# Expert layer on one core: first parameters ahead of the first gathers, later ones behind the scatter-adds, products begun with the first two chunks, the last full tiles by halves

## The chip, the cores and the metric

The kernel runs on one core of a Trainium2 chip. The metric is the device time of one execution in microseconds (us); less is better. Three executions of the kernel before took 483.40, 480.20 and 482.25 us, median 482.25. One further execution was profiled: 481.19 us, of which the span from the program's first instruction to its last is 479.5.

## The reference, cut to what matters

4096 tokens of 256 values pass through a mixture of 8 experts of three layers, and each token takes the two experts of the largest gate weights. All is float32.

```
var  = mean(x * x);  xn = rms_w * (x * rsqrt(var + 1e-6))
gate = xn @ wg_W + wg_b + (genre @ gg_W + gg_b)
w    = softmax(gate); the two largest are kept         # cw
h1   = relu(x @ W1[e] + b1[e])                         # 256 -> 512
h2   = relu(h1 @ W2[e] + b2[e])                        # 512 -> 512
out  = x + sum over the two experts of cw * (h2 @ W3[e] + b3[e])
```

## The kernel before

**Routing.** Tokens are sorted by expert, so that each expert is computed for its own tokens alone. The first 48 us work out the gates, choose two experts for each token, give every (token, expert) pair a slot and turn slots into tokens by products with one-hot matrices (L1167, eight batches of eight matmuls, `s_inv`). Behind each batch but the last stand four warm-up matmuls (`keep_busy(WARM_BATCH)`), behind the last one 96. The result is `tab_from` (L1001), the row of `x_ext` that each slot reads, and later `tab_to`, the row of the output that it adds to. `x_ext`, in DRAM, holds each token with its eight gate weights behind it; the gate weights (`dense`) are stored there by two DMAs that ACT's queue issues (L731), the token values by SP's queue.

**Experts are ranked by size.** `experts_of_tiles` (L966 to L979, VectorE, signal `s_names`) writes the rank of the expert of each tile into `etile`; rank 0 is the largest expert. Weights of rank 0 are loaded, scaled and split first. A float32 weight is split into two float16 parts: ScalarE writes the high part (`high_parts`, L716), VectorE the low part (`low_parts`, L825, two operations for each chunk). Each product is then three float16 matmuls (high by high, high by low, low by high). The activations are split in the same way (`split`, L1023 and L1025).

**Tiles.** 36 tiles of 256 slots follow. 32 of them have one expert each; three in the middle (29 to 31, `paired`) carry two experts of 128 slots each, whose weights are copied into `stage` (L1050), and the last, 35, is one half. One step of TensorE is, for tile i: layer two of tile i (48 matmuls of 256 columns), layer one of tile i+1 (24), the transposes of tile i+2 (four, L1182), layer three of tile i (24, L1260; by halves L1273, and L1286 in the last tile). Layer two waits for both halves of the split of `h1` (`s_h1`, `2 * i + 2`), layer three for both of `h2`. A half of a split is two of four chunks of 128 hidden units; ScalarE's activations (L770) deliver them chunk by chunk from the banks.

**The other engines in step i.** ScalarE: activations of layer two of tile i, of layer one of tile i+1, the high part of x for tile i+2, in some steps weight scales, high parts and sums of squares of a later expert, then the weighing of y (L780). VectorE: splits of both, the low part of x (L1012), in some steps two `low_parts`, then `finish` (L1030; by halves L1039), which takes y out of the bank. GpSimd: copies the table columns of tiles i and i+3 (L574), issues the two gathers of tile i+3 (L579), in some steps computes the parameters of a later expert (`parameters(late)`, L519 to L536, fourteen short operations linked by a semaphore), copies the parameters of tile i+2 (L588, awaited by the activations of its first layer), waits until tile i is weighed and the previous scatter-adds have landed, copies the gate weights of tile i+2 (L599) and issues the two scatter-adds of tile i to the output (L611). `PARAMETERS_AT` says in which step which rank is computed: ranks 1 to 7 in steps 0, 3, 6, 9, 12, 15 and 18.

**Start.** GpSimd waits for `x_ext` and `tab_from`, gathers tiles 0 and 1, computes the parameters of rank 0, waits for `s_names`, copies the parameters of both tiles and gathers tile 2. TensorE transposes tile 0 when its gathers have landed, runs 24 warm-up matmuls, layer one of tile 0, the transposes of tile 1, 24 more warm-ups, and enters step 0.

## Time and profile before

| | |
|---|---|
| median of three executions | 482.25 us |
| the profiled execution, its span | 481.19 us, 479.5 us |
| TensorE matmuls | busy 431.3 us, 90% of the span |
| VectorE, ScalarE, GpSimd | busy 306.3, 289.9 and 302.3 us |
| layers one and two, full tiles (L1226) | 2304 matmuls, ordinary spacing 0.109 us |
| layer three, full tiles (L1260) | 744 matmuls |
| scatter-adds (L611) | 71, mean 1679 ns, 3.9 us from issue to landing |
| gathers (L579) of tiles 3 on | 65, 3.0 us from issue to landing |

Times in the rows count from the start of the span. A matmul's recorded end is modelled and lies behind the start of the next, so a full TensorE is told by the starts. GpSimd's ends are rough. A value in square brackets is the idle time of the engine just before, with what ended it. Where one instruction waits for several semaphores, the wait is put down to the one that came last.

### The profile page before, as it was taken

What the parts mean: (1) busy time and instruction counts of PE and PEld (TensorE: products, weight loads), DVE (VectorE), ACT (ScalarE), POOL (GpSimd) and SP (SyncE); (2) the same over time, 40 slices, a digit from 0 to 9 for tenths busy, and PEclk for the clock granted to TensorE, in tenths of its full rate; (3) what the DMA queues carried; (4) which work ended last, traced back from release to release, by engine and by line L of the source; (5) the groups of instructions that cost most, each with busy time, mean ns of one, the idle gap of its engine ahead of it and who ended that gap; (6) DMA issues with size and microseconds to landing.
All of it is one profiled execution on the core that took longest, in us unless ns stands there. A gap on an engine that the chain in (4) does not pass through costs nothing.

```text
span 479.5 us, 13384 instructions
## 1 busy us (share of the span) xinstructions
PE 431.3 (90%) x4296; PEld 385.7 (80%) x4296; DVE 306.3 (64%) x531; ACT 289.9 (60%) x608; POOL 302.3 (63%) x457
## 2 busy tenths in 40 slices
PE   7606889999899999999999999899999999999980
PEld 6406768998689889888888998788899999899870
DVE  4898734776657756856856666555566667775550
ACT  6606529877578768778777764544555556554550
POOL 5720742757777776877877776766656666666451
PEclk9956989999899999999999999999999999999997
DMA  8989692555434544240444331322323433112221
GB/s 289 352 227 377 255 327 82 129 151 135 118 71 131 135 68 122 40 68 24 60 73 115 63 61 22 69 47 46 46 46 51 56 46 47 26 24 40 35 34 19
DMA packets 27179, 49.48 MB, mean 103 GB/s; under 512 B 8267, under 2 KB 21645, under 8 KB 24941
## 3 DMA queue, kind: packets, MB, share of 16 engines
q0 software_dynamic: 13632, 18.00, 22.9%
q1 hardware_dynamic: 9280, 30.45, 18.0%
q8 instruction: 42, 0.69, 0.6%
q10 hardware_dynamic: 4205, 0.17, 0.5%
q14 instruction: 20, 0.16, 0.1%
HBM read 40.08 MB, written 17.83 MB: 121 GB/s over the span
## 4 chain that ended last, share of the span: by engine, by line
PE 37%; POOL 26%; issue 12%; DVE 7%; ACT 5%; POOLq 4%; DMA 2%; DVEq 1%; SPq 0%; ACTq 0%
PE bank L1226 25%; POOL out L611 11%; PE bank L1260 7%; POOL area L579 5%; POOL bound L519 2%; ACT area L756 2%; DMA stage<-in_weights 1%; POOLq L597 1%; DVE area L1025 1%; PE bank L1202 1%; POOL cfrom L574 1%; DVE area L1023 1%; PE bank L1182 1%; ACT area L770 1%; PE bank L1273 1%
## 5 line engine op out<-in xcount | busy, mean ns | idle before, releaser
L1226 PE MATMUL bank<-area,w_hi 128*128 128x256 f16 x1536 | 257.0, 275 | 6.2 <-DVE area L1025 5.8
L1226 PE MATMUL bank<-area,w_lo 128*128 128x256 f16 x768 | 210.8, 274 | 0.0
L770 ACT ACTIVATE area<-bank,cprm 128x256 f32<-128x256 f32 (+1 forms) x264 | 132.3, 556 | 78.2 <-PE bank L1226 62.1
L1226 PEld LDWEIGHTS bank<-area,w_hi 128*128 x1536 | 150.7, 99 | 26.3 <-issue 8.2
L1023 DVE CAST area<-area 128x512 f16<-128x512 f32 (+1 forms) x144 | 66.1, 459 | 137.4 <-ACT area L770 127.1
L611 POOL DMA_INDIRECT out<-area,cto x71 | 119.2, 1679 | 41.9 <-issue 29.3
L1025 DVE TENSOR_TENSOR area<-area 128x512 f16<-128x512 f32 (+1 forms) x144 | 99.0, 688 | 5.0
L579 POOL DMA_INDIRECT area<-x_ext,cfrom x65 | 69.6, 1071 | 37.7 <-POOL cfrom L574 27.9
L1260 PE MATMUL bank<-w_hi,area 128*128 x496 | 86.3, 273 | 0.0
L1226 PEld LDWEIGHTS bank<-area,w_lo 128*128 x768 | 75.8, 99 | 9.3
L780 ACT ACTIVATE area<-area,cw 128x256 f32<-128x256 f32 x71 | 32.3, 500 | 71.0 <-DVE area L1030 52.7
L1260 PE MATMUL bank<-w_lo,area 128*128 x248 | 67.6, 273 | 0.0
L1260 PEld LDWEIGHTS bank<-w_hi,area 128*128 128x128 f16 x496 | 48.5, 98 | 5.3
L574 POOL COPY cto<-tab_to 128x2 int32<-128x2 int32 x36 | 33.0, 916 | 0.0
L599 POOL COPY cw<-area 128x2 f32 (+1 forms) x39 | 10.9, 282 | 33.4 <-ACT area L780 24.4
L1012 DVE SCALAR_TENSOR_TENSOR area<-bank,small,area 128x512 f16<-128x512 f32 x36 | 26.8, 746 | 3.1 <-ACT area L744 2.9
L744 ACT ACTIVATE area<-bank,small 128x512 f16<-128x512 f32 x36 | 24.9, 692 | 4.3 <-PE bank L1182 4.3
L574 POOL COPY cfrom<-tab_from 128x2 int32<-128x2 int32 x33 | 27.1, 820 | 0.0
L1202 PE MATMUL bank<-area,stage 128*128 128x128 f16 x432 | 25.1, 219 | 1.9 <-DVE area L1025 1.2
L1260 PEld LDWEIGHTS bank<-w_lo,area 128*128 128x128 f16 x248 | 24.3, 98 | 2.8
L1202 PEld LDWEIGHTS bank<-area,stage 128*128 128x128 f16 x432 | 24.4, 98 | 2.5 <-issue 2.4
L1182 PE MATMUL bank<-ident,area 128*128 128x128 f32 x142 | 21.6, 274 | 4.4 <-DMA area<-x_ext,cfrom 2.6
(199 smaller groups left out, 468.9 us busy)
## 6 DMA issues: line engine op xcount, KB each, us to landing
stage<-in_weights SPq DMA_DIRECT2D x10, 1024.0 KB, 6.0
area<-in_x SPq DMA_DIRECT2D x8, 512.0 KB, 7.5
x_ext<-in_x SPq DMA_DIRECT2D x8, 512.0 KB
out<-in_x SPq DMA_DIRECT2D x8, 512.0 KB, 6.9
w_lo<-in_weights SPq DMA_DIRECT2D x4, 1024.0 KB, 8.3
w_hi<-in_weights SPq DMA_DIRECT2D x2, 1024.0 KB, 9.0
out<-area,cto POOLq DMA_INDIRECT x71, 3.9
area<-x_ext,cfrom POOLq DMA_INDIRECT x65, 3.0
```

The costliest lines, as they stand in the source:

```text
L574: pool.tensor_copy(to, table[:, bass.ds(i * SUB, SUB)]).then_inc(signal, 1)
L579: pool.indirect_dma_start(out=xg[:, s, u, :], out_offset=None, in_=x_ext, in_offset=bass.IndirectOffsetOnAxis(ap=rows[:, u:u + 1].bitcast( ...
L611: pool.indirect_dma_start(out=out, out_offset=bass.IndirectOffsetOnAxis(ap=cto[:, s, u:u + 1].bitcast(U32), axis=0), in_=yb[:, s, u, :], i ...
L770: ins = act.activation(to[:, m * T + u * wide:m * T + (u + 1) * wide], ps_h[layer][b][:, a * T + u * wide:a * T + (u + 1) * wide], ACT.Rel ...
L780: act.activation(yb[:, slot, u, :], y32[:, u * H:(u + 1) * H], ACT.Copy, scale=cw[:, slot, u:u + 1]).then_inc(s_y, 1)
L1012: dve.scalar_tensor_tensor(xt_lo, ps_x[:, :], sx, xt_hi, ALU.mult, ALU.subtract).then_inc(s_xs, 1)
L1023: dve.tensor_copy(hi_b, h_b).then_inc(half_done, 1)
L1025: dve.tensor_tensor(lo_b, h_b, hi_b, ALU.subtract).then_inc(signal, 1)
L1182: ins = nc.tensor.transpose(ps_x[:, k * T + u * P:k * T + (u + 1) * P], xg[:, slot, u, k * P:(k + 1) * P], ident[:, :])
L1202: ins = nc.tensor.matmul(banks[u][:, m * P:(m + 1) * P], own[u][(0, 0, 1)[n]][:, at_own:at_own + P], xp[:, cols], start=(k == 0 and n == 0 ...
L1226: ins = nc.tensor.matmul(banks[m // 2][:, (m % 2) * T + u * wide:(m % 2) * T + (u + 1) * wide], weight, xp[:, cols], start=(k == 0 and n = ...
L1260: ins = nc.tensor.matmul(ps_y[:, u * H:(u + 1) * H], hp[:, cols], wp[:, bass.ds(w[u % len(w)] + (W3_AT + k * H), H)], start=(k == 0 and n ...
```

## The change

- **Parameters.** Rank 0's are computed before GpSimd waits for `x_ext` and `tab_from`, and tile 0's and 1's copies follow right behind the gathers of their tile. In the steps, the late parameters stand at the end, behind the scatter-adds; rank 1's move from step 0 to step 1.
- **Names.** The first four tiles (`FIRST`) take rank 0 as a constant, so that nothing waits for `s_names` before tile 4, and VectorE runs `experts_of_tiles` behind the low parts of the first expert instead of ahead of them.
- **Gate weights.** Their two stores to `x_ext` go from ACT's queue to SP's, behind the loads of rank 0's weights and bias and ahead of rank 1's.
- **Products.** Layer two of a full tile starts at the first half of `h1`: chunks 0 and 1 for output blocks 0 and 2, then, after the second half, the rest. Layer three does the same in all tiles but the paired ones: both halves of the tile with chunks 0 and 1, then both with 2 and 3. For that y lies in two banks.
- **End.** Tile 33 is finished, weighed and added by halves too.
- **Warm-up.** Four matmuls behind each of the first three batches only.

```diff
+FIRST = -(-LEAST // E)
-LOWS_AT, SQUARES_AT, SUMS_AT, HIGHS_AT, PARAMETERS_AT = {1: 2, 2: 3}, {}, {}, {0: 2, 1: 3}, {0: 1}
+LOWS_AT, SQUARES_AT, SUMS_AT, HIGHS_AT, PARAMETERS_AT = {1: 2, 2: 3}, {}, {}, {0: 2, 1: 3}, {1: 1}
...
-            return i + pair(i) + (1 if i > LAST - 1 else 0)
+            return i + pair(i) + max(0, i - (LAST - 2))
-            return paired(i) or i == LAST - 1
+            return paired(i) or i >= LAST - 2
...
-        bank = [ctx.enter_context(nc.psum_tensor(f"bank{b}", [P, 512], F32)) for b in range(8)]
+        bank = [ctx.enter_context(nc.psum_tensor(f"bank{b}", [P, 512], F32)) for b in range(5)]
+        y_banks = ctx.enter_context(nc.psum_tensor("y_banks", [P, SUB, 512], F32))
+        bank += [y_banks[:, u, :] for u in range(SUB)]
+        bank.append(ctx.enter_context(nc.psum_tensor("bank7", [P, 512], F32)))
...
# SP, behind b3_rows(e)
+                if e == 0:
+                    sp.wait_ge(s_dense, 1)
+                    for h in range(2):
+                        first = h * (N // 2 + 1)
+                        sp.dma_start(x_ext[first:first + N // 2, H:ROW].rearrange("(p j) e -> p j e", j=J),
+                                     je(dense)[h * P // 2:(h + 1) * P // 2]).then_inc(s_ext, 16)
...
# GpSimd, copy_parameters
+                if i == FIRST:
+                    pool.wait_ge(s_names, 1)
-                    e = pool.value_load(etile[0:1, bass.ds(name_at(i, u), 1)], min_val=0, max_val=E - 1)
+                    e = 0 if i < FIRST else \
+                        pool.value_load(etile[0:1, bass.ds(name_at(i, u), 1)], min_val=0, max_val=E - 1)
# GpSimd, step
-                if late is not None:
-                    link(parameters(late))
                 if i + 2 == PAIRED_AT:
                     pool.wait_ge(s_wsq, 4 * E)
...
                 add_rows(i, s)
-
+                if late is not None:
+                    link(parameters(late))
+
+            pool.wait_ge(s_whole, 1)
+            pool.wait_ge(s_order, 1)
+            link(parameters(0))
             pool.wait_ge(s_ext, (OUT_PARTS + 4) * 16)
             pool.wait_ge(s_from, 1)
             experts_of = []
             for i in range(RING):
                 gather(i, i, tab_from[:, i * SUB:(i + 1) * SUB])
-                if i == 1:
-                    pool.wait_ge(s_whole, 1)
-                    pool.wait_ge(s_order, 1)
-                    link(parameters(0))
-                    pool.wait_ge(s_names, 1)
-                    for n in range(2):
-                        experts_of.append(copy_parameters(n, n))
+                if i < 2:
+                    experts_of.append(copy_parameters(i, i))
...
# ScalarE, start
-            act.wait_ge(s_dense, 1)
-            for h in range(2):
-                first = h * (N // 2 + 1)
-                act.dma_start(x_ext[first:first + N // 2, H:ROW].rearrange("(p j) e -> p j e", j=J),
-                              je(dense)[h * P // 2:(h + 1) * P // 2]).then_inc(s_ext, 16)
...
# VectorE, behind tab_from
-            experts_of_tiles()
             low_parts(0)
+            low_parts(1, (0,))
             tables()
-            low_parts(1, (0,))
             x_low(0)
             low_parts(1, (1,))
+            experts_of_tiles()
             split(0, 0)
...
# TensorE
-                if b < BATCHES - 1:
+                if b < SUMS_BEHIND_BATCH:
                     keep_busy(WARM_BATCH, ones16[:, :], bank[6])
...
+                early, late = (0, 1), (2, 3)
+                pe.wait_ge(s_h1, 2 * i + 1)
+                products(*tile, 0, early)
+                products(*tile, 2, early)
+                pe.wait_ge(s_h1, 2 * i + 2)
+                products(*tile, 0, late)
+                products(*tile, 1, early + late).then_inc(s_l2, 1)
+                products(*tile, 2, late)
+                products(*tile, 3, early + late).then_inc(s_l2, 1)
...
# TensorE, start
-            pe.wait_ge(s_names, 1)
             layer1(0, weights_at(0))
```

`products` is new: it runs the three matmuls for each of the chunks `ks` into output block m. Layer three becomes what `layer3_last` was, with y in the two banks, for every tile that is not paired.

## Rows read from the trace of the kernel before

**Rows 1.** The page's first line.
```profile
span 479.5 us, 13384 instructions
```

**Rows 2.** Waits of TensorE: line <- releaser: us in total, times, longest.
```profile
PE bank L1226 <- DVE area L1025: 5.8, 7, 2.1
PE bank L1182 <- DMA area<-x_ext,cfrom: 2.6, 2, 1.7
```

**Rows 3.** Windows: stretch, length, busy time (count) by engine, clock, DMA share, GB/s.
```profile
54.00:55.80 1.80, 0.01 (x1) 0.01 (x1) 0.93 (x1) 0.01 (x1) 1.65 (x2) 1.00 0.32 94
66.30:69.70 3.40, 3.40 (x18) 2.42 (x17) 0.00 (x0) 0.08 (x1) 1.91 (x2) 0.50 0.90 301
122.24:124.20 1.96, 0.00 (x0) 0.00 (x0) 1.93 (x4) 1.93 (x5) 1.66 (x2) 1.00 0.01 1
124.35:127.70 3.35, 3.35 (x17) 2.42 (x16) 3.35 (x4) 0.99 (x2) 2.81 (x3) 0.50 0.59 74
303.18:304.85 1.67, 0.00 (x0) 0.00 (x0) 1.57 (x4) 1.11 (x3) 1.67 (x1) 1.00 0.27 51
```

**Rows 4.** Timeline of the front: start, us, engine, line, operation, [idle before].
```profile
27.69 5.39 ACTq L731 DMA_DIRECT2D x_ext<-area  x2
...
45.15 0.30 ACT L708 ACTIVATE scale<-expo,act_bias 128x3 int32<-128x3 int32 x1
...
48.04 0.23 DVE L1001 TENSOR_SCALAR tab_from<-bank 128x72 int32<-128x72 f32 x1 [1.90 <-PE bank L1167]
...
49.20 1.25 POOL L579 DMA_INDIRECT area<-x_ext,tab_from  x1 [19.35 <-DVE tab_from L1001]
...
50.44 2.48 DVE L825 SCALAR_TENSOR_TENSOR w_lo<-stage,scale,w_hi 128x1024 f16<-128x1024 f32 x2
...
50.75 1.79 POOL L579 DMA_INDIRECT area<-x_ext,tab_from  x1 [0.30 <-issue]
...
55.82 0.63 PE L1182 MATMUL bank<-ident,area 128*128 128x128 f32 x4 [1.81 <-DMA area<-x_ext,tab_from]
...
65.25 0.39 PE L1226 MATMUL bank<-area,w_hi 128*128 128x256 f16 x2 [2.11 <-DVE area L1025]
```

**Rows 5.** Timeline of GpSimd, step 0: first and last operation of `parameters`.
```profile
77.28 0.30 POOL L519 TENSOR_SCALAR bound<-fsq,small 128x1 f32<-128x1 f32 x1 [8.65 <-ACTq L710]
...
80.86 0.19 POOL L536 TENSOR_TENSOR prm<-prm,inv_scale 128x1 f32<-128x1 f32 x1
```

**Rows 6.** Timeline of step 1: weighing of tile 1 and its first scatter-add.
```profile
91.92 0.91 ACT L780 ACTIVATE area<-area,cw 128x256 f32<-128x256 f32 x2
...
94.63 1.79 POOL L611 DMA_INDIRECT out<-area,cto  x1 [0.40 <-issue]
```

**Rows 7.** Timeline of steps 15 to 17, GpSimd with its neighbours.
```profile
250.51 2.17 POOL L519 TENSOR_SCALAR bound<-fsq,small 128x1 f32<-128x1 f32 x1
...
253.35 0.91 ACT L780 ACTIVATE area<-area,cw 128x256 f32<-128x256 f32 x2
...
256.39 0.18 POOL L536 TENSOR_TENSOR prm<-prm,inv_scale 128x1 f32<-128x1 f32 x1
...
261.99 2.47 DVE L825 SCALAR_TENSOR_TENSOR w_lo<-stage,scale,w_hi 128x1024 f16<-128x1024 f32 x2
...
265.35 1.04 POOL L579 DMA_INDIRECT area<-x_ext,cfrom  x1 [0.85 <-POOL cfrom L574]
266.70 0.98 POOL L579 DMA_INDIRECT area<-x_ext,cfrom  x1 [0.31 <-issue]
...
269.80 0.60 PE L1182 MATMUL bank<-ident,area 128*128 128x128 f32 x4
```

**Rows 8.** Timeline of the end: layer three of tile 34, scatter-adds of tiles 34 and 35.
```profile
460.54 0.28 PE L1273 MATMUL bank<-w_hi,area 128*128 x1 [1.19 <-DVE area L1025]
...
464.34 1.58 POOL L611 DMA_INDIRECT out<-area,cto  x1 [2.94 <-DMA out<-area,cto]
...
470.87 1.55 POOL L611 DMA_INDIRECT out<-area,cto  x1 [2.90 <-ACT area L780]
```

More of the change, by code:

```diff
@@ L317, in build_moe @@
         ps_h = [[bank[0], bank[1]], [bank[2], bank[3]]]
[L318 to L320 removed]
+        ps_x, ps_y = bank[4], y_banks[:, :, 0:H]
         s_const = sem("s_const")
@@ L1241, in layer1 @@
                 pe.wait_ge(s_xs, i + 1)
-                layer(w, P if paired(i) else T, owned(i, 0), W1_AT, KH, (xt_hi, xt_lo), ps_h[0], s_l1,
-                      copied=(s_own1, pair(i) * SUB + 1), ready=[(s_xs, i + 1)] * 2 if two(i) else None)
+                own, copied = owned(i, 0), (s_own1, pair(i) * SUB + 1)
+                if two(i):
+                    halves_of_layer(own, KH, (xt_hi, xt_lo), ps_h[0], s_l1, copied, [(s_xs, i + 1)] * 2)
+                    return
+                if paired(i):
+                    pe.wait_ge(*copied)
+                tile = (w[0], halves_of(i) * P, own and own[0], W1_AT, KH, (xt_hi, xt_lo), ps_h[0])
+                for m in range(KM):
+                    ins = products(*tile, m, range(KH))
+                    if m % 2:
+                        ins.then_inc(s_l1, 1)
             def layer2(i, w):
@@ L1247, in layer2, with layer3_pair @@
                     wait_lows(pe, 1)
-                if not two(i):
-                    pe.wait_ge(s_h1, 2 * i + 2)
-                layer(w, P if paired(i) else T, owned(i, 1), W2_AT, KM, (h1_hi, h1_lo), ps_h[1], s_l2,
-                      copied=(s_own2, pair(i) * SUB + 1), ready=[(s_h1, 2 * i + 1 + u) for u in range(2)] if two(i) else None)
-            def layer3(i, w):
-                pe.wait_ge(s_h2, 2 * i + 2)
+                own, copied = owned(i, 1), (s_own2, pair(i) * SUB + 1)
+                if two(i):
+                    halves_of_layer(own, KM, (h1_hi, h1_lo), ps_h[1], s_l2, copied,
+                                    [(s_h1, 2 * i + 1 + u) for u in range(2)])
+                    return
+                if paired(i):
+                    pe.wait_ge(*copied)
+                tile = (w[0], halves_of(i) * P, own and own[0], W2_AT, KM, (h1_hi, h1_lo), ps_h[1])
+                early, late = (0, 1), (2, 3)
[7 more added lines that the diff above has]
+                products(*tile, 3, early + late).then_inc(s_l2, 1)
+            def layer3_pair(i, w):
                 pe.wait_ge(s_y32, pieces_before(i) + 1)
                 for u in range(SUB):
+                    pe.wait_ge(s_h2, 2 * i + 1 + u)
                     for k in range(KM):
```

70 lines of the change are left out of this document (23 added, 47 removed).

## The prediction

> **What bounds the kernel now.** I read the span first [rows 1], then the waits of TensorE alone [rows 2], then windows over each longer wait [rows 3]. The reader is to see that TensorE is the bound from tile 0's second layer on (65.25 [rows 4]) to the end: its second-layer products wait 5.8 us in all, in seven places, and its transposes 2.6 us, in two. Every other microsecond there can shrink only if a matmul is taken away, and the change takes none away in the tiles. So the change can win in three places: ahead of 65.25, in those few waits, and in the tail.
>
> A wait has a second price. The granted clock was 1.00 while TensorE stood from 122.24 to 124.20, and 0.50 for the next 3.4 us, all of them full of matmuls; the same after the 2.11 us before 65.25 [rows 3, 4]. At half of 2.4 GHz 3.4 us do the work of 1.7, so each cost 1.7 us more. Waits of 1.80 us (54.00) and 1.67 us (303.18) were followed by no fall [rows 3]. The Trainium skill (TensorE: Matmul & The Clock Gate, Part 1) says the gate follows how busy the array has lately been; by that a 1.7 us stall may cost nothing more or another 1.7, according to what lies around it. No run here varies it.
>
> The chain of waits behind those stalls is GpSimd's. One tile costs it two gathers, a copy of parameters and two scatter-adds; a step with `parameters(late)` costs it 3.8 us more when VectorE leaves it alone (77.28 to 81.05 [rows 5]) and 6.1 us when two of VectorE's low parts lie beside it (250.51 to 256.57; its first operation, 0.30 us elsewhere, took 2.17 [rows 5, 7]).
>
> **1. The front.** Parameters of expert 0 now come ahead of the first gather. They can start when ScalarE has the scales, 45.45 [rows 4], or up to 1 us sooner, since the store of the gate weights, whose issue ran until 33.08, no longer runs ahead of the weights; nothing to 1, taken 0.5. From about 45 to 46 VectorE makes one-hots; `tab_from` (48.04) comes earlier, since 12 warm-up matmuls between the last batches go: at most by the 1.90 that VectorE waited for those batches [rows 4], by 1.0 if each took 0.05 to 0.1, so at 47.1; and VectorE, which now leaves `experts_of_tiles` (48.27 to 50.44 [rows 4]) for later, starts its low parts at once: three of 1.24 us, 47.3 to 51. So parameters meet exactly the neighbour that slowed them at 250.51. Alone they would end at 49.3 and the first gather start at 50.2; with each low part holding up one operation they end near 52, and the gather starts near 53, against 49.20. The Trainium skill (SBUF — State Buffer, "Who interferes with whom") has the two engines share an exclusive lock held for a whole instruction, and advises putting on the far side of it whichever is off the critical path. By it this move is wrong, and 53 is the figure; without it 50.2.
>
> Before, the second gather (50.75) was found landed at 55.82, 5.1 us later, with weights in flight; the later steady ones need at most 3.1 (266.70 to 269.80 [rows 7]). A second gather at 54.3 lands after 3.1 to 3.7: 57.4 to 58. Transposes are then 1.6 to 2.2 us late. Against that, tile 0's first activation no longer waits for the parameter copy, and layer two starts when TensorE has issued what lies between: before, 2.11 of the 9.43 us from 55.82 to 65.25 were idle [rows 4]. 7.3 us after 57.7 is 65.0. `experts_of_tiles` has been put ahead of tile 0's split and ends it no later than that. Layer two thus starts 0.2 us earlier: I take zero. The clock: the 2.11 us wait and its 1.7 us go, but TensorE now stands some 4 us (53.5 to 57.7) instead of 1.8, longer than the waits that were followed by half a clock. I let the two cancel. Bounds: 3.8 us won (gather at 50.2, no fall of the clock) and 3.8 lost (gather later by another 2 us, clock lost twice).
>
> The store of gate weights, moved to SP's queue, took ACT's queue 5.39 us to issue [rows 4], with ScalarE waiting for weights anyway. On SP it stands behind expert 0's weights, so expert 1's and 2's are issued up to 5 us later. ScalarE takes expert 1's up after four conversions of expert 0's (some 4 us from 45.5): covered; without that cover, up to 2 us, inside the bounds. The first gather waits for this store too; at 53 it has landed. No wait for names before tile 4: nothing, cover ample.
>
> **2. Late parameters go behind the scatter-adds.** Take the step whose tile is weighed at 254.26 [rows 7]. In waiting steps the first scatter-add starts 1.8 us after the weighing (92.83 to 94.63 [rows 6]): 256.1. Two of 1.8 and 1.6 with a gap of 0.3 [rows 6, 8] end at 259.8. Parameters follow, then the next step's table copies (0.3), the gather's lead (0.85) and the second gather 1.35 behind the first [rows 7]. VectorE's next two low parts (261.99 to 264.46, about 1 us earlier in the new order) lie right on the parameters. So they end between 263.6 (3.8 us) and 265.9 (6.1); the second gather starts at 266.1 to 268.4, against 266.70; it lands 3.1 later, 269.2 to 271.5. TensorE wants it at 269.5 (269.80 less 0.3 of wait that goes). The stall is 0 to 2.0 us. The low parts are there in each cycle, so I go by the upper row, and take 1.5 because GpSimd's ends are rough and what follows a scatter-add begins before its recorded end.
>
> It recurs in all seven such steps (1, 3, 6, 9, 12, 15, 18), since each counts from the tile before: 10.5 us, and 0.5 for gathers that meet weights in flight: 11.0. It stands against what goes: tile 5's wait (1.96) with its clock (1.7), the other five waits of that line (5.8 - 2.1 - 2.0 = 1.7), of which starting with the first two chunks removes what the early copy of parameters would leave, and both transposes' waits (2.6), which turn into the new ones: 8.0. Net **+3.0**. What is queued behind the late parameters is the gather of tile i+4; before, it was the scatter-add of tile i, which nobody awaits.
>
> **3. First chunks first, y in two banks.** Same matmuls, 0.109 us apart. Layer two may start 1.1 us before its second split ends, layer three likewise. In the middle the waits it can take are already counted. Layer two's first half is signalled after 30 of 48 matmuls, not 24, hidden by the next tile's first layer.
>
> **4. The end.** The 1.19 us before tile 34's layer three go (460.54 [rows 8]). But the last scatter-add (470.87) waits for tile 34's to have landed as well as for its own tile; those start at 464.34, once tile 33's have landed and tile 34 is weighed. Tile 33 by halves frees the first condition by 1.5 us; the second moves 0.3 to 0.6, as VectorE still splits tile 35 in between. Won: 0.5 (0 to 1.3).
>
> **Sum**, from the profiled execution's own 481.2 (span 479.5): 0 + 3.0 - 0.2 (small waits among the pairs) - 0.5 = +2.3: **483.5**. That execution lies 1.1 us under the median of the runs.
>
> **Rivals.**
> - *GpSimd keeps up.* If parameters take nearer 3.8 us, the gathers land before 269.5 and the 8.0 us go for nothing: 481.2 - 8.0 - 0.5 = 472.7. For it: 3.8 is measured, and low parts may slip past. Against: at 250.51 they did not. 0.28.
> - *The stalls halve the clock* (slower). Place: transposes of tiles 5, 7, 10, 13, 16, 19, 22. It decides from stalls of about 1.96 us, seen to be followed by half a clock; 1.80 was not. At 2.0 us in seven places, three of them with 1.7 more: 14 + 5.1 - 8.5 = +10.6, 491.8; with one, 488.4. 0.22.
> - *The front decides*: late parameters neutral in total, front at either bound: 478 or 487. 0.05.
> - The forecast, 480 to 487: 0.45.
>
> **Numbers.** About 1% (4.8 us) is what a measurement tells from no change. Faster by more (under 477.4): the first rival, 0.28. Slower by more (over 487.1): most of the second, 0.22. Within: 0.50. Range 474 to 490: it leaves out the lower half of the first rival and the top of the second. The forecast's own is 480 to 487.
>
> **What would show it.** TensorE's waits: transposes waiting for gathers in about seven places, 1 to 2 us each, tile 5's layer-two wait gone. GpSimd: parameters of expert 0 ending near 52 and the first gather near 53; later ones of about 6 us, with single operations over 1 us. Clock at half near 57 instead of 66. I am wrong if transposes hardly wait (then fast), if parameters run in 4 us beside low parts, or if layer two of tile 0 starts more than 2 us from 65.

## The result, and the profile after

| | before | after |
|---|---|---|
| median of the runs, us | 482.03 (4 runs, 480.2 to 483.4) | 500.34 (4 runs, 497.32 to 501.82) |
| profiled execution, us (its span) | 481.19 (479.5) | 497.32 (495.7) |
| mean granted clock in it | 0.961 | 0.948 |

The ratio is 1.0374, 95% interval 1.0309 to 1.0439: slower by 18 us. The forecast was 483.5 with a range of 474 to 490, so it was wrong, and the time lies beyond even the rival that comes nearest (491.8). The profiled execution is the fastest of the four runs after; it shows 16.1 us of the 18. Ratios, here and below, leave out disturbed executions, so they can differ a little from those of the medians.

The page's first line of the kernel after, and TensorE's waits (line <- releaser: us in total, times, longest), against [rows 1, 2]:

```profile
span 495.7 us, 13085 instructions
```
```profile
PE bank L1188 <- DMA area<-x_ext,cfrom: 17.3, 7, 4.5
...
PE bank L1188 <- DMA area<-x_ext,tab_from: 5.9, 1, 5.9
...
PE bank L1212 <- DVE area L1031: 1.1, 1, 1.1
PE y_banks L1293 <- DVE area L1031: 0.9, 1, 0.9
```

The layer-two waits (5.8 us in seven places) are gone altogether. In their place the transposes (now L1188) wait for gathers seven times, 17.3 us. I followed them in the timeline of TensorE: 110.47 (2.31), 134.81 (1.92), 170.32 (2.18), 207.50 (2.18), 244.61 (2.11), 280.06 (2.12) and 319.17 (4.47), the transposes of tiles 5, 7, 10, 13, 16, 19 and 22, each the first that needs a gather issued behind late parameters.

Windows over two of them (stretch, length, then busy time and count for PE, PEld, DVE, ACT and POOL, clock, DMA share, GB/s), against [rows 3]:

```profile
108.16:110.47 2.31, 0.00 (x1) 0.01 (x1) 0.37 (x1) 1.42 (x4) 2.14 (x4) 1.00 0.32 93
110.47:113.90 3.43, 3.43 (x31) 3.13 (x32) 3.36 (x6) 3.25 (x6) 2.37 (x4) 1.00 0.51 58
...
168.14:170.32 2.18, 0.00 (x0) 0.00 (x1) 0.38 (x1) 1.43 (x4) 2.00 (x4) 1.00 0.31 103
170.95:174.70 3.75, 3.75 (x22) 2.73 (x20) 1.97 (x4) 3.39 (x6) 2.76 (x4) 0.54 0.63 70
```

Both times TensorE stands while GpSimd works. After 2.31 us the clock stays at 1.00 and 31 instructions pass in 3.43 us; after 2.18 us it is 0.54 on the mean of the next 3.75 us, and only 22 pass. Half clock (1.2 GHz) follows four of the seven waits: 3.4 us each behind those before 170.32, 207.50 and 280.06, and 6.8 us in one piece around the last, of which the first 1.1 us pass while TensorE still stands:

```profile
318.00:324.90 6.90, 5.73 (x27) 4.29 (x28) 3.03 (x5) 1.62 (x4) 5.22 (x7) 0.51 0.43 67
```

GpSimd in the step that answers to [rows 7] (start, duration, engine, line, operation, idle before):

```profile
258.91 1.19 POOL L601 COPY cprm<-prm 128x268 f32 x1
263.84 0.41 POOL L612 COPY cw<-area 128x2 f32 x1 [3.74 <-ACT area L786]
264.63 1.82 POOL L624 DMA_INDIRECT out<-area,cto  x1 [0.37 <-issue]
266.76 1.61 POOL L624 DMA_INDIRECT out<-area,cto  x1 [0.30 <-issue]
267.86 1.19 POOL L529 TENSOR_SCALAR bound<-fsq,small 128x1 f32<-128x1 f32 x1
...
269.51 1.29 POOL L531 TENSOR_TENSOR bound<-bound,fsq 128x1 f32<-128x1 f32 x1
270.98 1.02 POOL L532 TENSOR_TENSOR bound<-bound,small 128x1 f32<-128x1 f32 x1 [0.18 <-POOL bound L531]
...
274.27 0.19 POOL L546 TENSOR_TENSOR prm<-prm,inv_scale 128x1 f32<-128x1 f32 x1
...
275.90 1.10 POOL L589 DMA_INDIRECT area<-x_ext,cfrom  x1 [0.87 <-POOL cfrom L584]
277.30 0.95 POOL L589 DMA_INDIRECT area<-x_ext,cfrom  x1 [0.30 <-issue]
```
```profile
269.48 2.47 DVE L831 SCALAR_TENSOR_TENSOR w_lo<-stage,scale,w_hi 128x1024 f16<-128x1024 f32 x2
```
```profile
280.06 0.75 PE L1188 MATMUL bank<-ident,area 128*128 128x128 f32 x4 [2.12 <-DMA area<-x_ext,cfrom]
```

GpSimd first stands idle for 3.74 us, waiting for the weighing, and only then, with everything that the next gather needs long there, makes the parameters: 267.86 to 274.46, 6.6 us. The gather is issued behind them and lands 2.8 us after its second half is issued; TensorE had ended its work 2.12 us earlier. Tile 22's longer wait (4.47) has more in it, which I did not follow to its cause: the same tile waited in the kernel before (1.69 us before 304.87), its first scatter-add (302.65) starts 0.9 us later behind the copy of the gate weights than the one above, and its second gather takes 3.6 us to land.

The front, against [rows 4]:

```profile
29.14 0.17 PE L1166 MATMUL bank<-area,behind 128*128 128x8 f16 x1 [8.25 <-DVE area L923]
```
```profile
46.89 0.23 DVE L1007 TENSOR_SCALAR tab_from<-bank 128x72 int32<-128x72 f32 x1 [0.87 <-PE bank L1173]
47.04 3.66 DVE L831 SCALAR_TENSOR_TENSOR w_lo<-stage,scale,w_hi 128x1024 f16<-128x1024 f32 x3
47.29 1.08 POOL L487 TENSOR_SCALAR expo<-bound 128x2 int32<-128x2 int32 x1
48.45 1.11 POOL L489 TENSOR_SCALAR scale<-expo 128x2 int32<-128x2 int32 x1
49.65 1.12 POOL L493 TENSOR_SCALAR inv_scale<-expo 128x5 int32<-128x5 int32 x1
...
52.92 1.25 POOL L589 DMA_INDIRECT area<-x_ext,tab_from  x1 [0.55 <-POOL prm L546]
54.47 0.96 POOL L589 DMA_INDIRECT area<-x_ext,tab_from  x1 [0.30 <-issue]
...
58.88 1.08 PE L1188 MATMUL bank<-ident,area 128*128 128x128 f32 x4 [5.88 <-DMA area<-x_ext,tab_from]
...
66.96 0.27 PE L1227 MATMUL bank<-area,w_hi 128*128 128x256 f16 x1
```

Three low parts of 1.22 us, and beside them three operations of GpSimd of 1.08 to 1.12 us, 0.19 us elsewhere. Layer two of tile 0 starts at 66.96, 1.71 us later than before. The end, against [rows 8]:

```profile
482.57 0.28 PE L1293 MATMUL y_banks<-w_hi,area 128*128 x1 [0.89 <-DVE area L1031]
```
```profile
487.13 1.57 POOL L624 DMA_INDIRECT out<-area,cto  x1 [3.04 <-DMA out<-area,cto]
```

The first wait among the paired tiles, in the kernel before and after:

```profile
419.96 5.52 PE L1202 MATMUL bank<-area,stage 128*128 128x128 f16 x96 [1.16 <-DVE area L1025]
```
```profile
436.98 3.23 PE L1212 MATMUL bank<-area,stage 128*128 128x128 f16 x55 [1.12 <-DVE area L1031]
```

It moved by 17.0 us; the last scatter-add only by 16.3. The end won 0.8 us.

### The profile page after: what moved, and what is told of

It is laid out like the page before. It is cut to its first block, busy times and chain, and to the rows that moved or that the text cites. A ratio compares the mean times of both kernels' runs of the same rounds, so it can differ in the third digit from the quotient of the medians.

```text
span 495.7 us, 13085 instructions
## 1 busy us (share of the span) xinstructions
PE 436.7 (88%) x4280; PEld 389.4 (79%) x4280; DVE 306.3 (62%) x532; ACT 290.9 (59%) x608; POOL 300.0 (61%) x457
## 4 chain that ended last, share of the span: by engine, by line
PE 48%; POOL 14%; DVE 12%; issue 9%; DMA 8%; ACT 5%; POOLq 3%; SPq 0%; DVEq 0%; ACTq 0%
PE bank L1227 29%; PE y_banks L1293 10%; POOL out L624 4%; DVE w_lo L831 4%; DMA area<-x_ext,cfrom 3%; PE bank L1212 3%; PE bank L1188 2%; ACT area L776 2%; ACT area L786 2%; POOL bound L531 1%; DMA stage<-in_weights 1%; DVE area L1029 1%; PE bank L1113 1%; POOLq L610 1%; DVE area L1031 1%
## 5 line engine op out<-in xcount | busy, mean ns | idle before, releaser
L1227 PE MATMUL bank<-area,w_hi 128*128 128x256 f16 x1536 | 253.7, 273 | 0.0
L1227 PEld LDWEIGHTS bank<-area,w_hi 128*128 (+1 forms) x1536 | 150.3, 98 | 17.3
L624 POOL DMA_INDIRECT out<-area,cto x71 | 117.7, 1657 | 44.1 <-issue 25.3
L1293 PE MATMUL y_banks<-w_hi,area 128*128 (+1 forms) x520 | 97.9, 286 | 0.9 <-DVE area L1031 0.9
L1227 PEld LDWEIGHTS bank<-area,w_lo 128*128 (+1 forms) x768 | 75.1, 98 | 8.7
L1293 PE MATMUL y_banks<-w_lo,area 128*128 (+1 forms) x260 | 74.3, 286 | 0.0
L1293 PEld LDWEIGHTS y_banks<-w_hi,area 128*128 128x128 f16 x520 | 53.4, 103 | 9.3 <-issue 1.4
L1188 PE MATMUL bank<-ident,area 128*128 128x128 f32 x142 | 22.9, 285 | 23.2 <-DMA area<-x_ext,cfrom 17.3
L1188 PEld LDWEIGHTS bank<-ident,area 128*128 128x128 f32 x142 | 16.7, 145 | 25.7 <-DMA area<-x_ext,cfrom 19.3
L1018 DVE SCALAR_TENSOR_TENSOR area<-bank,small,area 128x512 f16<-128x512 f32 x36 | 26.8, 745 | 9.8 <-ACT area L750 9.8
L1036 DVE SCALAR_TENSOR_TENSOR area<-y_banks,cprm 128x512 f32<-128x512 f32 x30 | 22.3, 744 | 12.4 <-PE y_banks L1293 12.4
L1293 PEld LDWEIGHTS y_banks<-w_lo,area 128*128 128x128 f16 x260 | 26.7, 103 | 4.1
L584 POOL COPY cto<-tab_to 128x2 int32<-128x2 int32 x36 | 27.8, 772 | 0.4
```

The costliest lines, as they stand in the source:

```text
L584: pool.tensor_copy(to, table[:, bass.ds(i * SUB, SUB)]).then_inc(signal, 1)
L624: pool.indirect_dma_start(out=out, out_offset=bass.IndirectOffsetOnAxis(ap=cto[:, s, u:u + 1].bitcast(U32), axis=0), in_=yb[:, s, u, :], i ...
L1018: dve.scalar_tensor_tensor(xt_lo, ps_x[:, :], sx, xt_hi, ALU.mult, ALU.subtract).then_inc(s_xs, 1)
L1188: ins = nc.tensor.transpose(ps_x[:, k * T + u * P:k * T + (u + 1) * P], xg[:, slot, u, k * P:(k + 1) * P], ident[:, :])
L1227: ins = nc.tensor.matmul(banks[m // 2][:, (m % 2) * T:(m % 2) * T + wide], weight, xp[:, cols], start=(k == 0 and n == 0), stop=(k == chun ...
L1293: ins = nc.tensor.matmul(ps_y[:, u, :], hp[:, cols], wp[:, bass.ds(w[0] + (W3_AT + k * H), H)], start=(k == 0 and n == 0), stop=(k == KM - ...
```

## The experiments

The first theory is that of the rival, widened: late parameters between scatter-adds and gather make the seven stalls, and these halve the clock. Its rivals are the front and the new order of the products. The kernels compute the whole reference; each is timed against the kernel before on the same chip, and "ratio" is to that.

**1. `late_back`: the late parameters alone put back** (expert 1's at tile 0 again).

```diff
+                if late is not None:
+                    link(parameters(late))
                 if i + 2 == PAIRED_AT:
...
                 add_rows(i, s)
-                if late is not None:
-                    link(parameters(late))
```

> The changed kernel with the late parameters alone put back where they were (ahead of the copy of parameters, the first at tile 0); front, order of the products, y in two banks and end by halves stay as changed. If the place of the late parameters is the cause: the seven transposes' waits of about 2.2 us (15.3 with tile 22's 4.5) and the falls of the clock behind them go, 476 to 483 us. If the front or the order of the products costs the time, it stays at 490 or more.

Measured: 483.13 us, ratio 0.9999 (0.9965 to 1.0033). The 18 us are gone. The stalls are not all gone:

```profile
PE bank L1188 <- DMA area<-x_ext,cfrom: 8.1, 4, 3.7
```

The longest, 3.71 us before 135.91, is tile 7's. Layer two no longer waits, and the transposes wait 8.1 us where they waited 2.6 before. My reading, not tested by itself: TensorE reaches them sooner in the new order of the products, and cannot win what GpSimd is late by.

**2. `late_only`: the kernel before, with the late parameters behind the scatter-adds** (expert 1's at tile 1).

```diff
-                if late is not None:
-                    link(parameters(late))
                 if i + 2 == PAIRED_AT:
...
                 add_rows(i, s)
+                if late is not None:
+                    link(parameters(late))
```

> The kernel before with this one part of the change: late parameters behind the scatter-adds (expert 1's at tile 1). If their place is the cause: seven waits of the transposes near 2 us each and four to six falls of the clock of 1.7 us each appear, 494 to 503 us. If it needs the new order of the products or the new front as well, 482 to 487.

Measured: 499.96 us, ratio 1.0340 (1.0264 to 1.0415). One call moved makes nearly the whole loss, with the old front and the old order:

```profile
PE bank L1182 <- DMA area<-x_ext,cfrom: 17.2, 7, 4.5
```

The sum of its seven waits is that of the kernel after (17.3).

**3. `front_params_back`: the kernel after, with expert 0's parameters behind the second gather.**

```diff
-            pool.wait_ge(s_whole, 1)
-            pool.wait_ge(s_order, 1)
-            link(parameters(0))
...
+                if i == 1:
+                    pool.wait_ge(s_whole, 1)
+                    pool.wait_ge(s_order, 1)
+                    link(parameters(0))
```

> The changed kernel with the parameters of expert 0 back behind the second gather, the rest as changed. By my account of the front the later gather and the saved wait cancel: first gather near 49 instead of 52.9, layer two of tile 0 within 1.5 us of where it was, 497 to 503 us in all. If the front is the cause of the loss, under 490.

Measured: 499.34 us, ratio 1.0349 (1.0264 to 1.0433): as expected. But its trace shows another reason than the one I gave:

```profile
46.39 0.33 SPq L447 DMA_DIRECT2D w_lo<-in_weights  x1
```
```profile
51.53 1.80 POOL L589 DMA_INDIRECT area<-x_ext,tab_from  x1 [0.30 <-issue]
```

The second gather is issued at 51.53, 2.9 us sooner than in the kernel after (4.3 us, counted from the common event of experiment 9), and the transposes that need it start at 59.73, 8.2 us behind it. The store of the gate weights holds SP's queue until 43; the next weights are issued up to 46.39 instead of up to 38.84 as in the kernel before, and the early gathers share the DMA engines with them: those are busy to 0.97 or more from 52 to 58 us, in the kernel before to 0.79 from 52 to 54 and 0.29 from 54 to 56.

**4. `late_in_wait`: late parameters where GpSimd is idle, after the copy of parameters and ahead of the wait for the weighing.**

```diff
                     experts = copy_parameters(i + 2, s2)
+                if late is not None:
+                    link(parameters(late))
                 if not by_halves(i):
                     pool.wait_ge(s_y, 2 * i + 3)
...
                 add_rows(i, s)
-                if late is not None:
-                    link(parameters(late))
```

> The changed kernel with the late parameters between the copy of parameters of tile i+2 and the wait for the weighing, where GpSimd stands idle for about 3.7 us in a waiting step. If what costs is that the parameters stand whole between the scatter-adds and the next gather: they fill the idle time, scatter-adds and the next gathers move by 6.6 - 3.7 = 2.9 us or less instead of 6.6, which is 3.7 us sooner than now and more than the stalls of 2.2; the stalls go, and the layer-two waits stay gone through the early copy: 473 to 480 us. If any place after the copy is too late for the gathers, 488 or more.

Measured: 488.07 us, ratio 1.0115 (1.0030 to 1.0201). That is 8 us over the first expectation and at the edge of the second, and neither had the reason whole. Tiles 13, 16 and 19 no longer wait, as worked out; tiles 5, 7, 10 and 22 still do (2.85, 3.71, 1.82 and 1.92 us). The idle 3.7 us of one tile don't hold the 5.0 to 7.0 us that the parameters take here; only where GpSimd has more slack from the tiles around is there enough.

**5. `late_next_step`: late parameters of experts 2 to 7 one tile later, still behind the scatter-adds.**

```diff
-    PARAMETERS_AT[begin + 3] = rank
+    PARAMETERS_AT[begin + 4] = rank
```

> The changed kernel with the late parameters of experts 2 to 7 one tile later (behind the scatter-adds of tiles 4, 7, 10, ... instead of 3, 6, 9, ...), where VectorE has no low parts to make; expert 1's stay. If the 6.6 us that they take comes from sharing with VectorE's low parts, they take 3.8 to 4.4 us here, the gathers behind them come over 2 us sooner and the stalls of the transposes of tiles 8, 11, ... are under 0.5 us: 483 to 489 us. If they take 6 us or more without low parts beside them, the stalls only change place: 497 to 502.

Measured: 482.65 us, ratio 0.9989 (0.9957 to 1.0022): the loss is gone with the place on the engine unchanged. The parameters take 4.6 to 5.3 us here against 6.6 with low parts beside them; my 3.8 to 4.4 was too low. The slow operations that are left (0.91 and 0.55 us) lie at the start:

```profile
173.62 0.91 POOL L529 TENSOR_SCALAR bound<-fsq,small 128x1 f32<-128x1 f32 x1
...
175.86 0.55 POOL L532 TENSOR_TENSOR bound<-bound,small 128x1 f32<-128x1 f32 x1 [0.18 <-POOL bound L531]
176.49 0.19 POOL L487 TENSOR_SCALAR expo<-bound 128x2 int32<-128x2 int32 x1
```

So some 1.3 to 2.0 of the 6.6 us go with the low parts of VectorE. The stalls shrink from 17.3 to 7.7 us, in eight places. Three are over 1 us: 2.44 (expert 1's, which was not moved), 1.37 and 1.53; I had expected under 0.5 for the moved ones. Less than 2 us off each piece takes away most of the loss, since only what sticks out of GpSimd's slack stalls TensorE.

**6. `filled`: 36 matmuls of ones (`STAND`) while TensorE waits, in the kernel after.**

```diff
-                pe.wait_ge(s_xg[slot], (turn * SUB - SUB + halves_of(i)) * 16)
                 if i > 0:
                     pe.wait_ge(s_xs, i)
+                if i - 4 in PARAMETERS_AT:
+                    keep_busy(STAND, ones16[:, :], ps_x)
+                pe.wait_ge(s_xg[slot], (turn * SUB - SUB + halves_of(i)) * 16)
```

> The changed kernel with 36 matmuls of ones, 128 columns wide, ahead of the transposes of the seven tiles that wait (5, 7, 10, 13, 16, 19, 22), into the bank of the transposes. At 0.054 us each they fill 1.9 of the 2.2 us in which TensorE stands, and end before the gather lands. If the clock falls because TensorE stands, the five falls in the tiles go (three at least) and the time drops by 4 to 8.5 us with the gathers where they are: 489 to 496. If the falls have another cause, or the matmuls of ones cost what they save, 498 or more.

Measured: 495.70 us, ratio 1.0270 (1.0212 to 1.0328), 4.6 us less than the kernel after. The granted clock in the page, 40 slices of 12.4 us, as tenths; the kernel after first, then this one:

```profile
PEclk9956799999999999999999899889999999999997
```
```profile
PEclk8955789999999999999999999999999999999996
```

From the seventh slice on, the eights of the kernel after are gone, and only the last slice, in which TensorE has little work left, is below 9. The gathers come no sooner. So of 18 us some 5 came back with the clock. The five stretches at half clock in the kernel after cost about 8 (below); where the other 3 went I did not follow. Two waits stood behind the ones even so, 1.99 (before 247.73) and 2.64 us (before 320.86), and neither was followed by a fall.

**7. `products_only`: order of the products, y in two banks and end by halves alone.** Front and late parameters are those of the kernel before; against the kernel after it has the edits of experiments 1 and 3, and:

```diff
-                if e == 0:
-                    sp.wait_ge(s_dense, 1)
...
+            act.wait_ge(s_dense, 1)
...
+            experts_of_tiles()
             low_parts(0)
-            low_parts(1, (0,))
             tables()
+            low_parts(1, (0,))
             x_low(0)
             low_parts(1, (1,))
-            experts_of_tiles()
...
-                if b < SUMS_BEHIND_BATCH:
+                if b < BATCHES - 1:
```

> Order of the products, y in two banks and end by halves alone: front and late parameters as in the kernel before. By my sum these and the last tiles are worth 0.5 to 2 us for the end and what the waits of layer two turn into: 478 to 483 us, no difference that can be told. With the late parameters only put back the kernel stood at 483.1; if the new front were worth or cost several microseconds, this kernel would lie that much beside it.

Measured: 480.58 us, ratio 0.9883 (0.9835 to 0.9930). The median is as expected; the ratio puts it lower, at about 1% faster. Its one profile (span 480.0) shows three parts that nearly cancel. Counted as in experiment 9, layer two of tile 0 starts 1.1 us earlier than before (34.9 against 36.0), as it no longer waits for both halves of the split; from there to the paired tiles 1.9 us are lost, where the transposes of tile 7 now wait 3.90 us; the end wins 1.0. Where the 1% of the runs lies stays open. The long wait was not followed by half clock:

```profile
134.09:137.60 3.51, 3.51 (x32) 3.19 (x33) 0.75 (x1) 2.66 (x6) 2.35 (x5) 1.00 0.40 67
```

**8. `late_halves`: the late parameters cut in two, in the idle time of two tiles.**

```diff
+    for half in range(2):
+        PARAMETERS_AT.setdefault(begin + 3 + half, []).append((rank, half))
...
                     experts = copy_parameters(i + 2, s2)
+                for e, half in late:
+                    link(parameters(e, half))
```

> The changed kernel with the late parameters cut in two: seven operations (the bounds and their powers of two) between the copy of parameters and the wait for the weighing of one tile, the other eight at the same place of the next tile (expert 1 at tiles 0 and 1, the rest from tiles 3, 6, 9, ... on). Each part of about 3.3 us fits into the 3.7 us that GpSimd stands idle, so no gather moves. If GpSimd's lateness sets the stalls: those of 1.8 to 3.7 us that were left with the whole of them in one wait go or fall under 1 us, 474 to 481 us. If the early stalls (tiles 5 and 7) come from gathers that meet the weights' transfers, they stay: 483 or more.

Measured: 479.47 us, ratio 0.9917 (0.9884 to 0.9951). As expected, with 2.2 us left at tile 5, where I had hoped for under 1. The first part is six operations, the second eight:

```profile
119.05 0.30 POOL L531 TENSOR_SCALAR bound<-fsq,small 128x1 f32<-128x1 f32 x1
...
120.73 0.19 POOL L490 TENSOR_SCALAR scale<-expo 128x2 int32<-128x2 int32 x1
...
131.02 0.20 POOL L494 TENSOR_SCALAR inv_scale<-expo 128x5 int32<-128x5 int32 x1
...
132.66 0.19 POOL L548 TENSOR_TENSOR prm<-prm,inv_scale 128x1 f32<-128x1 f32 x1
```

Here it is 1.9 and 1.8 us, 3.7 together, what the whole costs when VectorE leaves it alone. The other six experts take 4.3 to 5.3 us together, in parts of 1.9 to 2.8, against 6.6 behind the scatter-adds.

**9. `front_only`: the kernel before, with the new front alone.** As in the change, with the gate weights' store, the names and fewer matmuls of ones; the core of it:

```diff
+            pool.wait_ge(s_whole, 1)
+            pool.wait_ge(s_order, 1)
+            link(parameters(0))
             pool.wait_ge(s_ext, (OUT_PARTS + 4) * 16)
...
+                if e == 0:
+                    sp.wait_ge(s_dense, 1)
...
             low_parts(0)
+            low_parts(1, (0,))
             tables()
```

> The kernel before with the new front alone: parameters of expert 0 ahead of the first gather, the gate weights' store on SP's queue behind expert 0's weights, names of the tiles later, fewer matmuls of ones. The other three runs suggest it costs 3 to 5 us (with late parameters back and new order 483.1, without the front as well 480.6): layer two of tile 0 then starts 20 us behind the last slot product instead of 17, 484 to 488 us. If it costs nothing, as I predicted, 480 to 484, and the new order of the products is what is worth nothing.

Measured: 487.32 us, ratio 1.0071 (1.0044 to 1.0098): 3.4 us by the ratio, 4.3 by the medians. Three operations of the parameters take 1.10 to 1.11 us again. TensorE's matmul of the counts and the start of layer two of tile 0:

```profile
31.39 0.17 PE L1162 MATMUL bank<-area,behind 128*128 128x8 f16 x1 [8.15 <-DVE area L919]
...
70.47 0.38 PE L1232 MATMUL bank<-area,w_hi 128*128 128x256 f16 x2 [0.25 <-DVE area L1027]
```

That matmul starts up to 4.2 us later in one profile than in another (28.8 to 33.0 us; I did not follow why), so I measure the front from it (29.24 in the kernel before) on:

| kernel | front | second gather issued | it landed | layer two of tile 0 |
|---|---|---|---|---|
| before | old | 21.5 | 26.4 | 36.0 |
| `products_only`, `halves_front_back` | old | 22.1, 21.1 | 27.0, 26.7 | 34.9, 34.4 |
| after | new | 25.3 | 29.6 | 37.8 |
| `front_only` | new | 25.9 | 29.9 | 39.1 |
| `front_params_back` | new, parameters late | 21.0 | 29.2 | 38.2 |
| `halves_store_back` | new, store on ScalarE's queue | 26.8 | 29.5 | 39.0 |
| `halves_params_early` | old, parameters early | 24.1 | 26.8 | 34.0 |
| `halves_lows_first` | old, low parts first | 20.8 | 26.9 | 35.2 |
| `halves_warm` | new, TensorE kept busy | 26.2 | 30.0 | 37.0 |

(us from that matmul; where no landing is recorded, the start of the transposes that wait for it, about 0.1 us later.) The five kernels with the whole new front that are not in the table lie at 38.0 to 39.1, the two with the old front at 36.8 (`late_only`) and 35.0 (experiment 12). The profiled execution of the kernel after, at 37.8, is the best of those with the new front, but for `halves_warm`: the one that I compared first flattered the front. And it has the new order of the products, which starts layer two 1.1 us sooner: its 1.7 us over the kernel before hide a dearer front. Like against like it costs 3.1 us in the old order (39.1 against 36.0) and 2.8 to 4.7 in the new (37.8 to 39.1 against 34.4 to 35.0).

The front costs something behind it too: in its profile `front_only` takes 1.9 us more from layer two of tile 0 to the end than the kernel before (416.1 against 414.2). The transposes of tiles 7, 10 and 22 wait 2.34, 2.08 and 1.54 us, and 3.4 us at half clock lie at each of the first two; in the kernel before only tile 22's wait over 1 us.

**10. `halves_store_back`: `late_halves` with the store back on ScalarE's queue.**

```diff
+            act.wait_ge(s_dense, 1)
+            for h in range(2):
+                first = h * (N // 2 + 1)
+                act.dma_start(x_ext[first:first + N // 2, H:ROW].rearrange("(p j) e -> p j e", j=J),
+                              je(dense)[h * P // 2:(h + 1) * P // 2]).then_inc(s_ext, 16)
```

> The kernel with the late parameters cut in two, and the gate weights' store back on ScalarE's queue, the rest of the new front kept. If the store on SP's queue is what makes the front dear (it holds the next weights' issue back by 6 us, so that they are still in flight beside the first gathers, which take 4.2 us to land): the weights are issued near 36 again, the second gather lands within 3.1 to 3.5 us, and the time falls by 1 to 3 us against the 479.5 of that kernel, 476 to 479. If the parameters ahead of the gather are what costs, it stays at 479 to 481, with the first gather at 53.

Measured: 479.29 us, ratio 0.9924 (0.9893 to 0.9956); no difference to `late_halves` can be told. The gather does land 2.8 us after it is issued, but it is issued as late as ever, behind the parameters.

**11. `halves_front_back`: `late_halves` with the whole old front.** This is the combination that the runs so far point to. It is `late_halves` with the edits of experiments 3 and 7 for the front.

```diff
                 if i == 1:
                     pool.wait_ge(s_whole, 1)
                     pool.wait_ge(s_order, 1)
-                    link(parameters(0))
+                    for half in range(2):
+                        link(parameters(0, half))
```

> The kernel with the late parameters cut in two and the whole front as before: gathers near 50 again, layer two of tile 0 some 3 us sooner and one fall of the clock fewer. If front and late parameters add up: 479.5 less 3 to 5, 474 to 477 us. If what the front gives is lost in the stalls of tiles 5 and 7, where GpSimd is still behind from its start: 478 to 481.

Measured: 473.96 us, ratio 0.9794 (0.9755 to 0.9833). By the ratio it is 2.1% under the kernel before (1.7 to 2.5, so whether it is over 2% isn't settled), and by the medians 5.3% under the kernel after. TensorE's waits for gathers:

```profile
PE bank L1191 <- DMA area<-x_ext,cfrom: 3.3, 5, 1.0
PE bank L1191 <- DMA area<-x_ext,tab_from: 2.7, 1, 2.7
```

**12. `one_tile_later`: old front, new order, late parameters whole at their old place, one tile later.** On `products_only`:

```diff
-    PARAMETERS_AT[begin + 3] = rank
+    PARAMETERS_AT[begin + 4] = rank
```

> Front as before, new order of the products, whole late parameters at their old place (behind the gather) but one tile later, where VectorE makes no low parts, so that they take 3.8 instead of 6.1 us. If the rest of the stalls (3.9, 2.4 and 1.8 us at the transposes of tiles 7, 10 and 22 with the old tiles) comes from the operations that wait for low parts: they shrink to 1.5 us at most, 475 to 479 us. If GpSimd is late for other reasons, 480 to 483.

Measured: 474.61 us, ratio 0.9829 (0.9792 to 0.9865). One constant changed is worth about what cutting in two is (6.0 us by the medians, against `products_only`); the parameters take 4.5 to 5.1 us, and no wait of the transposes in the tiles is over 0.84.

Open then was why the front costs what it does, as neither the store nor the parameters moved back by themselves had changed the time.

**13. `halves_params_early`: `halves_front_back` with expert 0's parameters ahead of the gathers.**

```diff
+            pool.wait_ge(s_whole, 1)
+            pool.wait_ge(s_order, 1)
+            for half in range(2):
+                link(parameters(0, half))
             pool.wait_ge(s_ext, (OUT_PARTS + 4) * 16)
```

> The kernel with the late parameters cut in two and the front as before (473.96), with one part of the new front: the parameters of expert 0 and their copies ahead of and between the first gathers. VectorE begins with the experts' names (2.2 us), so fewer of its low parts lie beside them, but the first gather still stands behind all of them: if they are what makes the front dear, second gather 2 to 3 us later, 476.5 to 479. If the front is dear only where they meet low parts, under 475.

Measured: 473.24 us, ratio 0.9828 (0.9770 to 0.9887). With the experts' names first, no low part lies beside the parameters until 51.22:

```profile
46.92 0.29 POOL L525 TENSOR_SCALAR bound<-fsq,small 128x1 f32<-128x1 f32 x1 [16.45 <-ACTq L718]
...
48.59 0.19 POOL L484 TENSOR_SCALAR scale<-expo 128x2 int32<-128x2 int32 x1
...
51.17 0.19 POOL L542 TENSOR_TENSOR prm<-prm,inv_scale 128x1 f32<-128x1 f32 x1
51.91 1.71 POOL L585 DMA_INDIRECT area<-x_ext,tab_from  x1 [0.55 <-POOL prm L542]
```

The parameters take 4.4 us instead of 6.5. The second gather lands within 2.7 us; the DMA engines' share is 1.00 from 51 to 53 us and 0.38 from 53.9 to 56.7, so most of the weights ahead of it have landed by then. This front is the shortest of all (34.0).

**14. `halves_lows_first`: `halves_front_back` with the other half of the new front.**

```diff
-            experts_of_tiles()
             low_parts(0)
-            tables()
             low_parts(1, (0,))
+            tables()
             x_low(0)
             low_parts(1, (1,))
+            experts_of_tiles()
...
-                if b < BATCHES - 1:
+                if b < SUMS_BEHIND_BATCH:
```

> The kernel with the late parameters cut in two and the front as before (473.96), with the other part of the new front: VectorE's low parts ahead of the tables and of the experts' names, and twelve matmuls of ones fewer between the slot products; parameters of expert 0 and the gate weights' store where they were. If the parameters alone make the front dear: 472.5 to 475, the table about 1 us sooner. If the order of VectorE's work or the clock at the slot products does: 477 or more.

Measured: 475.69 us, ratio 0.9873 (0.9798 to 0.9949). Between the two expectations. The time is told apart neither from `halves_front_back` (0.9794) nor from `late_halves` with the whole new front (0.9917), but in its profile layer two starts at 35.2, by the old front's 34.4 and not by the new one's 38.0. So by the profiles neither half alone makes the front dear; both at once do.

**15. `halves_warm`: `late_halves` (new front) with 190 matmuls of ones ahead of the first transposes.**

```diff
-WARM_TILES = 96
+WARM_TILES = 190
```

> The kernel with the late parameters cut in two and the whole new front (479.5), with 190 instead of 96 matmuls of ones ahead of the first transposes, so that TensorE stands under 1 us there instead of 6.2. If half of the front's cost is the second 3.4 us at half clock behind that wait: the fall near 62 is gone, 1.5 to 3.5 us less, 476 to 478. If the clock falls there in any case, 479 to 481.

Measured: 473.67 us, ratio 0.9810 (0.9751 to 0.9868), 5.8 us less than `late_halves`: more than I had expected. The wait is 0.91 us instead of 6.2, and there is no fall behind it. In the profiles that is worth 0.9 us up to layer two and 1.7 us behind it. The profiled execution (477.20) is 3.5 us over the median, so it shows only part of the gain; I did not find the rest. The parameters meet the low parts here as before (7.3 us), so what this run takes away is only TensorE's long wait and the half clock behind it.

## Why the prediction was wrong

- **Bound and places: right.** TensorE sets the time from tile 0's second layer on, and the seven new stalls stand at the tiles that were named.
- **Front, taken at 0: wrong by 3.4 to 4.3 us** (1.7 in the one profile, where 1.1 us won by the new order of the products hides a part). The mechanism was right: parameters ended at 52.38, first gather 52.92 ("near 52", "near 53"). What failed is "I let the two cancel" and "7.3 us after 57.7": the gather landed at 58.75, and from there to layer two it took 8.2 us, because transposes, matmuls of ones and the first products ran at half clock after a wait of 5.88 us. The fall of the clock was in my text and stood at nothing in the sum. Experiments 9, 10, 13 and 14 point to the collision of low parts and parameters as what starts it, and experiment 15 wins as much by keeping TensorE busy with the collision left in. How the cost divides between the later gather and the clock behind the wait is open. The Trainium skill (SBUF — State Buffer, "Who interferes with whom"), by which VectorE and GpSimd share a lock that one holds for a whole instruction, was the right guide here: the rows show operations of 0.19 us taking 1.1 beside low parts of 1.2.
- **Late parameters: right in kind, the term was mis-sized.** I had 3.8 to 6.1 us for them; they took 6.6 (experiments 5 and 8: 4.6 to 5.3 one tile later, 3.7 to 5.3 in two cuts). A stall was taken at 1.5 of a range of 0 to 2.0; six measured 1.9 to 2.3, and tile 22's 4.5. That is 17.3 instead of 11.0, 6.3 us short. At the upper bound or over it throughout: where each term of a sum recurs seven times from one cause, a value short of that bound is a poor choice, for all seven err together.
- **Clock behind the stalls: left out of the forecast, priced only in the rival.** Half clock for three times 3.4 us and once 5.7 behind the waits in the profile of the kernel after, which is about 8 us lost; filling the waits gave 4.6 back. The rival's condition ("decides from stalls of about 1.96 us") does not hold: 2.31, 2.11, 2.64, 2.68 and even 3.90 us were followed by no fall, 2.12 and 2.18 were. The Trainium skill (TensorE: Matmul & The Clock Gate, Part 1) has the gate follow how busy the array has lately been. The traces agree so far that the length of one wait does not decide it and that filling the waits removed every fall in the tiles.
- **What goes, 8.0 us: right.** Layer two's waits and both waits of the transposes went, into the new ones.
- **End, -0.5: right** (-0.8).
- **Order of the products, 0:** by one comparison of runs it gives about 1%. Its profile shows 1.1 us won at layer two of tile 0, which the sum had at nothing, and lost again in the tiles.
- **The sum on the profiled execution:** front +1.7; from layer two of tile 0 to the paired tiles +15.3, that is 17.3 of stalls less 8.0, and about 8 of clock less the 1.7 that before lost behind 66.3 (15.6 by these); end -0.8. In all +16.2, the difference of the spans.
- **Chances.** 0.22 for the case that came, against 0.45 and 0.28 for cases whose middle values lay on the low side of what the rows allowed. "At 250.51 they did not" was written down against the fast rival and should have weighed against the forecast too.

## What to carry to other kernels

Ask of the engine that issues gathers not only how long a moved piece takes but how much idle time it has, and on which side of it the piece stands. Here GpSimd is idle for 3.7 us per tile, waiting for the weighing. A piece of 6.6 us behind that wait cost TensorE about 2.1 us each time; the same piece in two cuts of 1.9 to 3.1 us ahead of it left no wait for a gather above 1.0 us in the tiles (experiment 11). Work on GpSimd and on VectorE that both can place freely should be kept apart in time: shifting one by a tile was worth 17.7 us behind the scatter-adds and 6.0 us at the old place. A wait of about 2 us of the bounding engine should be priced with its clock, as a range from nothing to 1.7 us more.

## What the runs showed of the hardware

- Small operations of GpSimd (0.19 us) take 1.1 us beside VectorE's `w_lo` operations of 1.2 us, one at a time: the parameters take 3.8 us in one piece alone and 6.6 us beside those and the splits.
- The same wait may or may not halve the clock: no stretch at half clock after 2.31, 2.64, 2.68 and 3.90 us, one of 3.4 us after 2.12 and 2.18, either after 1.99 (one in the kernel before, none in `filled`), one of 6.8 us, begun during the wait, with 4.47 and with 5.88.
- A gather of 128 rows behind the first ones lands 2.7 to 3.1 us after its issue (`halves_params_early`, `halves_store_back`); with weights in flight the first gathers took 4 to 6 us, and 8.2 in `front_params_back`.
- The matmul of the counts starts at 28.8 to 33.0 us in the seventeen profiles, so two profiles of fronts are best compared from a common event.
